# Expert outputs of a two-layer token model: weighted when they leave PSUM and added to token rows in DRAM by chained accumulating scatters, in place of gathers per token

## The reference

```python
# layer 0: E=15 experts, TOPK=3; layer 1: E=32 experts, K=4; D = F = 256
logits = xt @ gate_w.T                                 # (2056, E)
scores = softmax(logits)
topk_w, topk_idx = top_k(scores, TOPK)
topk_w = topk_w / sum(topk_w)
comb[token, expert] = topk_w                           # zero elsewhere
h = xt @ fc1_w[e] + fc1_b[e];  a = gelu(gate) * linear # per expert
y = a @ fc2_w[e] + fc2_b[e]
out = x + sum_e comb[:, e] * y[e]                      # plus a shared expert in layer 0
```

## Time and profile before

| | us |
|---|---|
| median of three runs | 2078.4 |
| profiled execution | 2077.95 |
| its span in the trace | 2076.1 |
| routing, layer 0 (from 472 to 572) | 100 |
| experts, layer 0 (572 to 801) | 229 |
| projections with combine, layer 0 (801 to some 950) | 149 |
| routing, layer 1 (1561 to 1649) | 88 |
| experts, layer 1 (1649 to 1983) | 334 |
| output phase, layer 1 (1983 to 2076) | 93 |

### The profile page before, as it was taken

One profiled execution on the slowest core, in us unless ns is written; L12 is line 12 of the kernel. 1 busy time (PEld: TensorE's weight loads), 2 busy tenths in 40 slices (PEclk: granted clock), 3 DMA queues, 4 the chain that ended last, 5 costly groups with the idle time before them and its releaser, 6 DMA issues. The chain is left out here.

```text
span 2076.1 us, 38819 instructions
## 1 busy us (share of the span) xinstructions
PE 1464.4 (71%) x13394; PEld 1239.7 (60%) x13394; DVE 1088.6 (52%) x3452; ACT 590.4 (28%) x1444; POOL 598.5 (29%) x743
## 2 busy tenths in 40 slices
PE   0599786992979983662875556999941599898831
PEld 0599564772768882442764434777741588888720
DVE  8960444337323332552369954777257565565534
ACT  0000332110033331010477633666230033333300
POOL 6430000002333334870620021110110733333256
PEclk9999997995589997676998868999755599999965
DMA  0000001000089994442226685454010189999933
GB/s 27 1 1 1 16 0 34 23 16 3 1 267 319 321 308 131 103 116 74 62 98 255 271 295 153 155 175 129 1 42 9 69 289 322 313 327 308 304 110 110
DMA packets 147184, 288.43 MB, mean 139 GB/s; under 512 B 33144, under 2 KB 114484, under 8 KB 145012
## 3 DMA queue, kind: packets, MB, share of 16 engines
q1 hardware_dynamic: 122356, 250.82, 35.8%
q0 software_dynamic: 24704, 35.93, 6.2%
HBM read 216.17 MB, written 70.35 MB: 138 GB/s over the span
## 5 line engine op out<-in xcount | busy, mean ns | idle before, releaser
L1199 PE MATMUL ex_pg<-ex_xT,ex_w 128*128 128x128 f32 x1280 | 179.5, 284 | 48.0 <-DMA ex_w<-in_m_w 35.0
L1199 PEld LDWEIGHTS ex_pg<-ex_xT,ex_w 128*128 128x128 f32 x1280 | 158.4, 195 | 66.6 <-ACT ex_xT L1233 30.4
L1170 POOL DMA_INDIRECT ex_xg<-moe_rows,ex_idx x160 | 155.8, 974 | 127.4 <-POOL ex_idx L1167 126.7
L1741 PE MATMUL bi_ps<-bi_pos,bi_spread 64*32 64x128 f32 x4128 | 139.1, 290 | 65.1 <-ACT bi_spread L1751 49.8
L334 PE MATMUL s_ps<-s_x,s_q 64*64 64x32 f32 x1024 | 129.9, 311 | 73.0 <-DVEq L286 73.0
L334 PEld LDWEIGHTS s_ps<-s_x,s_q 64*64 64x64 f32 x1024 | 129.7, 222 | 73.0 <-DVEq L286 73.0
L1199 PE MATMUL ex_pl<-ex_xT,ex_w 128*128 128x128 f32 x1280 | 171.6, 278 | 0.0
L1741 PEld LDWEIGHTS bi_ps<-bi_pos,bi_spread 64*32 64x32 f32 x4128 | 120.1, 115 | 84.0 <-ACT bi_spread L1751 59.9
L1208 PE MATMUL ex_py<-ex_w,ex_mid 128*128 128x256 f32 x640 | 165.0, 380 | 1.0 <-DVE ex_mid L1297 0.6
L1199 PEld LDWEIGHTS ex_pl<-ex_xT,ex_w 128*128 128x128 f32 x1280 | 158.3, 195 | 0.0
L2170 ACT ACTIVATE a_pr<-a_sc,a_nm 128x257 f32<-128x257 f32 x256 | 115.6, 500 | 100.9 <-DVE a_nm L2126 100.6
(11 more groups left out here) (347 smaller groups left out, 2848.1 us busy)
## 6 DMA issues: line engine op xcount, KB each, us to landing
ex_w<-in_m_w SPq DMA_DIRECT2D x160, 771.0 KB, 5.9
a_bt<-attn_bias SPq DMA_DIRECT2D x64, 516.0 KB, 5.9
attn_bias<-bi_T SPq DMA_DIRECT2D x14, 2322.0 KB, 7.9
moe_y<-ex_y SPq DMA_DIRECT2D x160, 128.0 KB, 5.5
ex_xg<-moe_rows,ex_idx POOLq DMA_INDIRECT x160
attn_v<-pj_v SPq DMA_DIRECT2D x8, 274.1 KB
a_v<-attn_v SPq DMA_DIRECT2D x8, 272.0 KB, 7.2
moe_rows<-mi_tn SPq DMA_DIRECT2D x17, 128.0 KB, 1.7
```

The costliest lines, as they stand in the source:

```text
L1170: nc.gpsimd.indirect_dma_start(xg[r][:], None, m.rows.rearrange("t p d -> (t p) d"), bass.IndirectOffsetOnAxis(idx[r][:], 0)).then_inc(x_i ...
L1199: last = nc.tensor.matmul(banks[q][:, 0, f * P:(f + 1) * P], up(r, c, f0 + f), xT[q][:, c], start=c == 0, stop=c == KC - 1)
L1741: last = nc.tensor.matmul(ps[s % 4][g * MB:(g + 1) * MB, i // 3, (i % 3) * NBK:(i % 3 + 1) * NBK], spread[s % 2][rw, c, i], pos[rw, table, ...
```

## The change

`m.y` and its store, `gslot`, the 72 + 68 gathers of the combine and the weighted additions are gone. In their place:

- Routing builds a second half of `hot_t`, in which the token number is replaced by the weight: ScalarE scales each `hot_t` row by `ratio` = weight / token number. The product on TensorE is 2M wide (128 and 192 columns) and gives `idcols` and a weight per slot, `wcols`. The softmax weights are computed before the ranks. Token numbers start at 1, empty slots get spare rows of their own. GpSimd zeroes a tile and SyncE writes it over a DRAM table of sums, `m.sums`.
- Experts: ScalarE's eviction scales by `wcols`. GpSimd scatters tile t to `m.sums` with an accumulating indirect DMA, after the gather of tile t+7, and after it has waited for the eviction of t and for the completion of the scatter of t-1. The index copies go.
- Combine: per image one plain DMA of `m.sums` and one addition.

```diff
+        self.table = nc.dram_tensor(f"moe{n}_rows", (self.NT * self.TS + ETILE, D), F32).ap()
+        self.sums = nc.dram_tensor(f"moe{n}_sum", (self.NR, D), F32).ap()
@@ routing_phase
+            sp.wait_ge(zeroed, 1)
+            sp.dma_start(m.sums.rearrange("(p n) d -> p (n d)", p=P), zero[:]).then_inc(cleared, 16)
+            sp.dma_start(m.table[NT * TS:], zero[:, 0:D]).then_inc(cleared, 16)
+            sp.wait_ge(cleared, 16 * 2)
...
+            G.memset(zero[:], 0.0).then_inc(zeroed, 1)
-            pool.wait_ge(c_in, 16 * 7)
+            pool.wait_ge(c_in, 16 * 8)
...
             dve.sem_inc(mask_ready, 1)
+            (the block of softmax weights, L1035 to L1048, moved here)
+            own(V.reciprocal(ratio[:], tok[:].unsqueeze(2).to_broadcast([TS, NT, K])))
+            own(V.tensor_tensor(ratio[:], ratio[:], wts[:], ALU.mult))
 
             dve.wait_ge(rank_ps, 1)
...
-            V.tensor_copy(gslot[:], slot[:])
...
+            dve.wait_ge(ids_ps, 1)
+            V.tensor_copy(wcols[:], pid[:, 0, M:2 * M])
+            own(V.tensor_scalar(lost[:], pid[:, 0, 0:M], 0.0, spare[:], ALU.is_equal, ALU.mult))
+            own(V.scalar_tensor_tensor(idcols[:], pid[:, 0, 0:M], -1.0, lost[:], ALU.add, ALU.add))
             if m.first:
                 dve.sem_inc(add_b2.comb_ready, 1)
@@ scalar
-            act.wait_ge(ids_ps, 1)
-            nc.scalar.activation(idcols[:], pid[:, 0, 0:M], ACT.Copy).then_inc(ids_ready, 1)
+            for t in range(NT):
+                act.wait_ge(hot_odd if t % 2 else hot_even, t // 2 + 1)
+                for k in range(K):
+                    last = nc.scalar.activation(hot_t[:, t, k, 1], hot_t[:, t, k, 0], ACT.Copy, scale=ratio[:, t, k:k + 1])
+                last.then_inc(hot_w, 1)
@@ tensor
-                    last = nc.tensor.matmul(pid[:, 0, 0:M], hot_p[:, t, k], hot_t[:, t, k],
+                    last = nc.tensor.matmul(pid[:, 0, 0:2 * M], hot_p[:, t, k], hot_t[:, t, k].rearrange("p z m -> p (z m)"),
@@ experts_phase
-            def store(i, r):
-                sp.wait_ge(y_ready, t + 1)
-                sp.dma_start(m.y[bass.ds(t * ETILE, ETILE)], y[r][:]).then_inc(y_out[r], 16)
...
+            LAG = 7
+            def gather(t):
                 free(pool, xt_ps, t - 3)
-                nc.gpsimd.tensor_copy(idx[r][:], idcols[:, bass.ds(t, 1)]).then_inc(idx_ready, 1)
+                nc.gpsimd.indirect_dma_start(xg[t % R][:], None, m.table,
+                                             bass.IndirectOffsetOnAxis(idcols[:, t:t + 1], 0)).then_inc(x_in[t % R], 16)
+            def scatter(t):
+                pool.wait_ge(y_ready, t + 1)
+                if t >= 1:
+                    pool.wait_ge(y_out[(t - 1) % R], 16 * ((t - 1) // R + 1))
+                nc.gpsimd.indirect_dma_start(m.sums, bass.IndirectOffsetOnAxis(idcols[:, t:t + 1], 0), y[t % R][:], None,
+                                             compute_op=ALU.add).then_inc(y_out[t % R], 16)
+            for t in range(M + LAG):
+                if t < M:
+                    gather(t)
+                if t >= LAG:
+                    scatter(t - LAG)
...
-                A_(y[r][:], py[q][:, 0, 0:D], ACT.Copy).then_inc(y_ready, 1)
+                A_(y[r][:], py[q][:, 0, 0:D], ACT.Copy, scale=wcols[:, t:t + 1]).then_inc(y_ready, 1)
...
-            with act.Fori(1, NI - 1) as i:
+            for i in range(1, NI - 1):
@@ Combine (project_phase)
+    def loads(self, pool):
+        for b in range(B):
+            if b >= 2:
+                pool.wait_ge(self.added, b - 1)
+            self.nc.gpsimd.dma_start(self.yg[b % 2][:], self.m.sums[b * SP:(b + 1) * SP].rearrange(
+                "(u p) d -> p u d", p=TS)).then_inc(self.y_in[b % 2], 16)
     def add(self, dve, own, b, q, h):
+        dve.wait_ge(self.y_in[q], (b - q) * 8 + 16)
+        self.nc.vector.tensor_tensor(rows, rows, self.yg[q][:], ALU.add).then_inc(self.added, 1)
@@ output_phase (R = 3, g over 9 groups)
+                add_b2.add(dve, g)
+                dve.wait_ge(add_b2.b_done, g + 1)
+                dve.wait_ge(y_in[g % R], 16 * (g // R + 1))
+                V.tensor_tensor(rows, rows, yg[g % R][0:n, 0:w], ALU.add).then_inc(added, 1)
...
+            def load(g):
+                sp.dma_start(yg[g % R][0:n, 0:w], m.sums[UT * g * RT:UT * g * RT + w * n].rearrange(
+                    "(u p) d -> p u d", p=n)).then_inc(y_in[g % R], 16)
```

More of the change, by code:

```diff
@@ L1156, in _ @@
                     load(i, r)
[L1157 to L1160, removed]
         @block.gpsimd
         def _(pool):
-            def gather(i, r):
-                t = R * i + r
+            LAG = 7
+            def gather(t):
                 free(pool, xt_ps, t - 3)
-                nc.gpsimd.tensor_copy(idx[r][:], idcols[:, bass.ds(t, 1)]).then_inc(idx_ready, 1)
[L1168 to L1171, removed]
-            for r in range(R):
-                gather(0, r)
-            with pool.Fori(1, NI) as i:
-                for r in range(R):
-                    gather(i, r)
-            for r in range(R):
-                pool.wait_ge(x_in[r], 16 * NI)
+                nc.gpsimd.indirect_dma_start(xg[t % R][:], None, m.table,
[11 more added lines that the diff above has]
+                    scatter(t - LAG)
+            for r in range(R):
+                pool.wait_ge(y_out[r], 16 * NI)
         @block.tensor
@@ L1341, in output_phase, with __init__ @@
-def output_phase(nc, h, ident, m, wts, gslot, comb, out):
-    R, T, K = 6, m.NT, m.K
+    OWN = 0
+    def __init__(self, nc, ph, m):
+        self.nc, self.m = nc, m
+        self.yg = [ph.sb(f"yg{q}", [TS, IT, D]) for q in range(2)]
+        self.y_in = [ph.sem(f"y_in{q}") for q in range(2)]
+        self.added = ph.sem("added")
+    def loads(self, pool):
[4 more added lines that the diff above has]
+                "(u p) d -> p u d", p=TS)).then_inc(self.y_in[b % 2], 16)
@@ L1344, in output_phase @@
+    def add(self, dve, own, b, q, h):
+        rows = h[:, bass.ds(b * IT, IT), :] if not isinstance(b, int) else h[:, b * IT:b * IT + IT, :]
+        dve.wait_ge(self.y_in[q], (b - q) * 8 + 16)
+        self.nc.vector.tensor_tensor(rows, rows, self.yg[q][:], ALU.add).then_inc(self.added, 1)
+def output_phase(nc, h, ident, m, comb, out):
+    R, T = 3, m.NT
     with Phase(nc, "out") as ph:
-        yg = [ph.sb(f"yg{r}", [RT, K, D]) for r in range(R)]
+        yg = [ph.sb(f"yg{r}", [RT, UT, D]) for r in range(R)]
@@ L1346, in output_phase, with shape @@
         y_in = [ph.sem(f"y_in{r}") for r in range(R)]
-        added, own_v, stored = ph.sem("added"), ph.sem("own_v"), ph.sem("stored")
+        added, stored = ph.sem("added"), ph.sem("stored")
         add_b2 = AddB2(nc, ph, m, ident, comb, h)
         block = ph.block()
-        def count(t):
-            return RT if t < T - 1 else B
-        @block.gpsimd
-        def _(pool):
-            for t in range(T):
-                n = count(t)
-                free(pool, added, t - R + 1)
-                for k in range(K):
-                    nc.gpsimd.indirect_dma_start(yg[t % R][0:n, k], None, m.y,
-                                                 bass.IndirectOffsetOnAxis(gslot[0:n, t, k:k + 1], 0)
-                                                 ).then_inc(y_in[t % R], 16)
+        def shape(g):
+            return (RT, UT) if g < B else (B, 1)
@@ L1364, in _ @@
         @block.vector
         def _(dve):
[L1366 removed]
+            V = nc.vector
             dve.sem_inc(add_b2.comb_ready, 1)
[L1368 to L1380 removed]
+            for g in range(B + 1):
+                n, w = shape(g)
+                rows = h[0:n, UT * g:UT * g + w, :]
+                add_b2.add(dve, g)
+                dve.wait_ge(add_b2.b_done, g + 1)
+                dve.wait_ge(y_in[g % R], 16 * (g // R + 1))
+                V.tensor_tensor(rows, rows, yg[g % R][0:n, 0:w], ALU.add).then_inc(added, 1)
@@ L1548, in _ @@
                 nc.gpsimd.memset(v[q][:], 1.0).then_inc(v_ones, 1)
-            comb.gathers(pool)
+            comb.loads(pool)
         @block.vector
@@ L1579, in step @@
                 last.then_inc(v_ready, 1)
-            pairs(own.loop(B // 2 - 2, 2 * (norm.OWN + comb.OWN * (m.K - 1)), first=1), step)
+            pairs(own.loop(B // 2 - 2, 2 * (norm.OWN + comb.OWN), first=1), step)
         @block.scalar
```

147 lines of the change are left out of this document (56 added, 91 removed).

## The result

The changed kernel takes 2334.1 us (median; 2330.3 to 2337.9), the kernel before beside it 2075.8 (2067.0 to 2084.3): ratio 1.1239, 95% interval 1.1202 to 1.1276. It is slower by 258 us where 208 were forecast (2286); 2334 lies in the range of 2060 to 2560. The profiled execution has a span of 2336.0 us.

What follows compares the result with a forecast made beforehand. Prediction: TensorE and DMA together bound the experts, GpSimd's gather issue the combines. From 2078.0 us, plus 313 for chained scatters, minus 66 and 46 for the combines, plus 7 routing: 2286 us; range 2060 to 2560.

Steps and rivals of the forecast that it cites:

- rival A: Expert stages: chained scatters 4.2 to 5.9 us apart, total 2126 to 2398 us, 2286 at 5.2; chance 0.58 together with D.
- P: Expert stages: time from one scatter to the next, forecast 5.2 us, plus 313 us in all; break-even at 3.9 us.
- L: Expert stages: landing time of a scatter after its time on GpSimd, taken as 3.9 us between 1.9 and 6.1.
- rival C: Expert stages: completion within 2.6 us of GpSimd's end, chain hides under a tile; 2048 us, or 1981; chance 0.16.
- seven tiles early: Expert stages: gathers queued behind a waiting scatter are seven tiles early, so TensorE doesn't starve for them.
- First scatter and fill: Expert stages: first scatters at 594 and 1669 us, after gather 7; the initial fill is counted in the plus 313 us.
- Projections: Layer 0 combine: without gathers, images 11.2 us apart for 15.7 and start 14 us earlier; minus 46 us (minus 30 to minus 60).
- D: Combines: they give less because 256 KB loads collide with stores of q, k, v and h; at most 27 us more.
- Output: Layer 1 combine in the output phase: 68 gathers go, groups of 2.0 us; minus 66 us (minus 55 to minus 69).
- Routing: Routing of both layers: softmax before the ranks, wider products and more copies; plus 7 us (0 to plus 20).
- Clock: Expert stages: a sign of being right, TensorE's clock falls from 0.97 towards 0.7.
- rival B: Expert stages: slower scatters or a lower TensorE clock; 2414 us at the low clock, 2638 with L = 6.1; chance 0.26.

Runs made afterwards that it cites:

- the second occasion: The changed kernel run once more with nothing edited: 2313.6 us, ratio 1.115 to the kernel before.
- noweights: Changed kernel with weights loaded only for the first four tiles and used for all, chain kept: 2189.2 us.
- plain: Changed kernel with scatters that write their rows instead of adding them, chain of waits kept: 2156.8 us.
- nogather: Changed kernel with token rows gathered only for the first four tiles and used for all, chain kept: 2338.0 us.
- ownrows: Changed kernel with each tile adding into one of four own row sets, no wait for the last scatter, sums by token left out: 2022.8 us.
- split: Changed kernel, one table, with layer 0 projections' 86-partition stores of h and v and table loads cut into 80 and 6: 2251.3 us, ratio 1.080 to before.
- three_split: Changed kernel with three tables by turns, scatter t waiting for t-3, and 86-partition transfers cut into 80 and 6: 1983.6 us, ratio 0.954 to before.

## Why the prediction was right

The mechanism was rival A's. Its main signs are in the trace: evictions waiting for `y_out`, scatters over 4.2 us apart, expert stages of 369 and 547 us (355 and 520 forecast), DMA share 0.68. Other signs came differently: the distance of the scatters is not even, the clock fell less, the projections' images are 7.5 to 13.7 us apart, and one sign against the forecast came as well. The time is 48 us above the forecast's. By its terms:

- **P**, forecast 5.2, measured 5.45 and 5.48 (5.31 on the second occasion). The right size hides three errors. GpSimd's part was taken from a gather, 0.97; an accumulating scatter is 1.59. The prediction listed "over 1.5 us on GpSimd itself" as a sign against itself, and this came. The wake was 0.35 with the issue, and is 0.68. L was taken as 3.9; the flight behind GpSimd's end is 2.5 in the middle and some 3.2 on the mean (5.46 - 1.59 - 0.68). So two parts were 0.95 too short and one 0.7 too long, and P came within 0.25 to 0.28: that is luck. In sum 1.59 + 2.5 + 0.7 = 4.8, the median gap; the late third brings the mean to 5.46. With the true flight and the rest as forecast, P would have been 3.8 by the median (0.30 + 0.97 + 2.5 + 0.05), at the break-even, and 4.5 by the mean. The flight of 2.6 us from which rival C decides was met in half of the cases, and the chain bound all the same. *noweights* and *plain* show the parts.
- **Gathers "seven tiles early"**: they are not. At 1905.22 GpSimd issues the gather whose rows the transposes at 1910.08 wait for, and such waits are TensorE's longest (239 us). The forecast did not suffer by it, since *nogather* takes the gathers away and P stays.
- **First scatter and fill**: 18.1 and 16.3 us into the stages for the forecast 21.3 and 19.4, together 6 us less.
- **Close of the stages**, P + 1 forecast behind the last scatter's start, so 6.2 us; measured 8.0 (931.43 to 939.4) and 10.6. After GpSimd's last completion its queue drains, and the barrier waits. Before, this drain (7.9 us) ran from 1965.9 on beside the last tiles and ended 9 us before the phase did. It is a cover that the prediction did not notice, 6 us in all (3.2 us of drain in layer 0, and in layer 1):

```profile
L100 POOLq DRAIN  x2: 34/2756/5479, 2309.0 to 2315.5; - x2
```

  Together: 0.25 x 63 + 0.28 x 95 = 42, minus 6, plus 6: 42, for the 41 us by which the experts missed.
- **Bytes of the addition**: 0.43 a tile for rival C, or nothing if they lie in gaps. Measured between the two: a tile of *ownrows* is 0.13 (layer 0) and 0.17 us (layer 1) longer than one of the kernel before. Rival C's lower price, 1981, should be 1979 by its own terms.
- **Projections**, minus 46 forecast, minus 28 measured. The step that failed is "the next limit is TensorE's own round", 11.2 us. That round was read in the kernel before at the low clock (six transposes took 1.09 us, here 0.61 in the second to fourth image); without waits it is 7.5 us, and SyncE's stores are the limit, 13.5 us. By luck the mix of both gives 11.2 on the mean ((1036.64 - 958.42)/7), so the 32 us of this term came. The 18 us are lost elsewhere: 11 behind the last image's transposes, where the stores still run (38.5 us for 27.1 before), and 7 at the start. The prediction gave D 27 us for colliding DMAs. It didn't look at SyncE's issues of the 86-partition stores, which GpSimd's 15.5 us per image had covered. *split* shows it. The start was late: first transposes 19 us into the phase for the forecast 12.4 (before 26.6), because the first load, issued at 940.84, was added only at 953.48, 12.6 us later. The forecast had 5.8, with 4.1 to land taken from a gather.
- **Output**, minus 66 forecast, minus 72.5: a group took 1.5 us for 2.0. **Routing** right within 1 us.
- **Clock**, forecast to fall "towards 0.7": 0.86 to 0.88. Low stretches follow the long waits. At 1910.56, after TensorE had waited 3.49 us for a gather, eight entries took 2.04 us (granted clock 0.50, so 1.2 GHz), against 1.06 at 1903.78 (1.00, so 2.4 GHz) and again at 1916.02. The whole round at the low clock took 5.7 us (1910.08 to 1915.80), close to the 5.8 that rival B named as the ceiling, though its rows give 5.5 (3.04 x 1.91/1.06). No stage stayed at it, and the experts of *ownrows* and *three_split* stand at 0.98 to 1.00.

```profile
1903.78 1.06 PE L1212 MATMUL ex_pg<-ex_xT,ex_w 128*128 128x128 f32 x8
...
1910.56 2.04 PE L1212 MATMUL ex_pg<-ex_xT,ex_w 128*128 128x128 f32 x8
...
1916.02 1.06 PE L1212 MATMUL ex_pg<-ex_xT,ex_w 128*128 128x128 f32 x8
```

- **Rival C** was right in part about the gaps in the bytes and wrong about the completion. It needed the next scatter 3.9 us after the last; the least with a nearly idle memory is 4.3 (4.29 in *noweights*).

## What to carry to other kernels

Where each DMA must wait for the last one's completion, as here, they have a rate of one per whole round trip (engine time, flight, wake), whatever the byte rate leaves free. Work that round trip out, from the mean and not the median, and compare it with the length of a tile; if it is longer, put N independent destinations in turn, until N tiles last longer than one round trip. Here two tables turn a loss of 12% into a gain of 1%, and the cut stores into 4%. When a slow engine is taken off a stage, look next at every queue that it covered: the queue of stores here, the drain at the phase's end.

## What the runs showed of the hardware

- An accumulating scatter of 128 rows of 1 KB takes 1.59 us of GpSimd, a plain one 0.99; the flight behind it is nearly the same (2.5 and 2.3 us).
- Beside the weights' transfers a chained scatter lands in 3.6 to 4.1 us in half of the cases and in up to 8.2 in the rest; without the weights' transfers never over 3.9.
- With unchained accumulating scatters in place of plain stores, the middle of layer 1 ran at a DMA share of 0.99 and 296 GB/s of counted bytes, for 0.96 and 321 before. A tile took 3.46 us for 3.29.
- Issues of 258 KB stores with 86 partitions occupied SyncE for 5.0 us in the middle (4.0 in the kernel before); those of the same bytes in 80 and 6 partitions 0.33 each.
